# Layer 1 of a two-layer graph network: SyncE brings every 42nd chunk's rows

## The reference, cut to what matters

```python
N, E, D, R = 3750, 120000, 256, 8
h = relu(layernorm(x))                          # [N, D]
x = x + attention_layer(h, src, dst, type)      # layer 0: softmax over a node's incoming edges
h = relu(layernorm(x))
h_all = einsum('ni,rio->nro', h, W)             # [N, 8, 256]: one row for each (node, relation)
msgs = h_all[src, type]                         # one row of 256 floats (1 KB) for each edge
agg = segment_sum(msgs, dst)                    # summed by target node
g = gelu(agg + h @ loop_w + h_bias + h)
x = x + layernorm(g) * gamma + beta
```

## Time and profile before

| | us |
|---|---|
| median of 3 runs | 3214.21 |
| lowest and highest run | 3211.46, 3218.01 |
| span of the profiled execution, first to last instruction | 2765.4 |
| layer 1 within it, from POOL's first gather to the end | 1538.0 to 2765.4 |
| POOL, PE, DVE busy, whole span | 2027.0, 1916.5, 1521.9 |

### The profile page before, as it was taken

One profiled execution on the slowest core, in us unless ns is written; L12 is line 12 of the kernel. 1 busy time (PEld: TensorE's weight loads), 2 busy tenths in 40 slices (PEclk: granted clock), 3 DMA queues, 4 the chain that ended last, 5 costly groups with the idle time before them and its releaser, 6 DMA issues.

```text
span 2765.4 us, 26428 instructions
## 1 busy us (share of the span) xinstructions
PE 1916.5 (69%) x8092; PEld 1421.7 (51%) x8092; DVE 1521.9 (55%) x3172; ACT 672.9 (24%) x1246; POOL 2027.0 (73%) x2137
## 2 busy tenths in 40 slices
PE   7993577887878778787887656565655656565564
PEld 6992355555555555555555444444444444444443
DVE  6765677787777778777877423323332333333233
ACT  3753323443443344344331100000000000000001
POOL 5866777777777777777774577777777777777775
PEclk9995689899899999989999877768677776877777
DMA  8557456556565655656553533333333333333333
GB/s 224 228 195 233 137 151 177 168 173 179 163 183 169 177 168 172 179 163 185 169 161 89 170 105 105 105 110 105 110 107 109 111 105 110 105 110 110 106 111 94
DMA packets 168504, 403.11 MB, mean 146 GB/s; under 512 B 49741, under 2 KB 75820, under 8 KB 160682
## 3 DMA queue, kind: packets, MB, share of 16 engines
q0 software_dynamic: 95312, 261.58, 34.9%
q1 hardware_dynamic: 73050, 139.85, 14.5%
HBM read 325.41 MB, written 75.86 MB: 145 GB/s over the span
## 4 chain that ended last, share of the span: by engine, by line
POOL 49%; issue 18%; PE 17%; DVE 12%; DMA 3%; ACT 0%; DVEq 0%; POOLq 0%; ACTq 0%; SPq 0%
POOL Z L857 49%; PE PB L1910 7%; PE PB L1862 5%; DVE Z L1397 3%; DMA Z<-tab,KI 3%; DVE ACC L1369 3%; PE PB L2028 3%; PE PB L1986 1%; PE PB L1970 0%; PE PB L2071 0%; DVE EV L1411 0%; DVE E L1414 0%; DVE RV L1433 0%; DVE sf L1444 0%; POOL Z L805 0%
## 5 line engine op out<-in xcount | busy, mean ns | idle before, releaser
L857 POOL DMA_INDIRECT Z<-tab,KI x1963 | 1870.3, 953 | 658.7 <-issue 576.6
L1910 PE MATMUL PB<-Z,OHZ 128*128 128x260 f32 (+1 forms) x3926 | 1253.7, 484 | 528.2 <-DMA Z<-tab,KI 388.7
L1910 PEld LDWEIGHTS PB<-Z,OHZ 128*128 128x128 f32 x3926 | 941.3, 248 | 784.3 <-DMA Z<-tab,KI 415.2
L1369 DVE TENSOR_TENSOR ACC<-ACC,PB 128x260 f32 (+1 forms) x997 | 421.7, 423 | 851.6 <-PE PB L1910 826.5
L1397 DVE TENSOR_TENSOR Z<-Z,PB 128x2048 f32<-128x2048 f32 (+1 forms) x125 | 283.8, 2271 | 0.0
L2028 PE MATMUL PB<-w,ht 128*128 128x512 f32 x448 | 218.5, 644 | 12.8 <-ACT ht L1788 12.8
L1842 ACT ACTIVATE ACC<-ACC 128x256 f32<-128x256 f32 x30 | 10.4, 405 | 772.9 <-DVE ACC L1369 772.9
L1660 ACT ACTIVATE sd<-ve 128x1 f32<-128x1 f32 (+2 forms) x52 | 10.6, 203 | 660.7 <-DVE ve L1617 403.2
L2028 PEld LDWEIGHTS PB<-w,ht 128*128 128x128 f32 x448 | 89.3, 204 | 124.7 <-issue 105.5
L1862 PE MATMUL PB<-wh,hx 128*128 128x424 f32 (+1 forms) x500 | 145.1, 362 | 1.0 <-ACT hx L1674 1.0
L1387 DVE TENSOR_TENSOR OHZ<-DL,PB 128x1024 f32<-128x1024 bf16 (+1 forms) x122 | 140.2, 1210 | 0.1
(11 more groups left out here) (352 smaller groups left out, 1662.2 us busy)
## 6 DMA issues: line engine op xcount, KB each, us to landing
OHZ<-dlt SPq DMA_DIRECT2D x31, 1024.0 KB
Z<-tab,KI POOLq DMA_INDIRECT x1963, 2.8
tab<-st SPq DMA_DIRECT2D x120, 256.0 KB, 3.8
tab<-Z SPq DMA_DIRECT2D x24, 1040.0 KB, 4.1
TD<-typ SPq DMA_DIRECT2D x31, 256.0 KB
tab<-Z SPq DMA_DIRECT2D x5, 1024.0 KB, 7.2
xn<-xb SPq DMA_DIRECT2D x30, 128.0 KB, 3.3
X<-xn SPq DMA_DIRECT2D x6, 640.0 KB, 9.8
```

Source lines behind the costliest of these rows:

```text
L857: pool.indirect_dma_start(to, None, tab, at).then_inc(d_fe[g % 2][part(g, k) * layer], 16)
L1369: dv.tensor_tensor(a, a, bank(done + i)[:, 0:width], ALU.add).wait_op(*previous, "sem-ge").then_inc(*o.of(s_add))
L1910: last = pe.matmul(p, OH[:, slot, k + i, :], rows_, start=(i == 0), stop=(i == n - 1))
```

## The change

`BY_SP` is 46, 88, 130, ..., 928: 22 chunks. POOL leaves them out (`absent`). SP fetches each of them by 128 transfers of one row, from an address that stands in a register, to one partition of `LAND`, two tiles that lie over the first two rows of `rows`. The addresses are the keys in `ERM`, turned into integers and shifted left by 10 (1024 bytes a row) by two new DVE operations; SP loads 16 of them at a time. SP waits until PE has used the chunk brought two before. After a chunk's rows it stores those output blocks whose scaling falls in an earlier group than the chunk's; the rest are stored at the end. PE reads those chunks' rows from `LAND` and waits for them by a semaphore of their own, one of four.

```diff
+BY_SP = list(range(46, END1 - G, 42))
+    tab1b = tab1.rearrange("q f -> (q f)").bitcast(U8)
+        LAND = over("land", [128, 2, D], F32, rows_at)
+        KR = ERM[:, :].bitcast(I32)
+        def scaled_in(b):
+            return next(NB + 2 if then is None else then for a, c, ready, at, then in ENDS if a <= b < c)
         def absent(k):
-            return k < UNITS[0][0]
+            return k < UNITS[0][0] or k in BY_SP
+        def landed_by_sp(k):
+            i = BY_SP.index(k)
+            return d_sp[i % 4], 16 * 128 * (i // 4 + 1)
+        def row_bytes(e, engine, k, a, n):
+            return nc.values_load_multi_w_load_instructions(
+                KR[k % 128:k % 128 + 1, 128 * (k // 128) + a:128 * (k // 128) + a + n], engines=[engine], min_val=0, ...)[1]
         def rows1(g, k):
-            return FE[:, g % 2, k, 0:D]
+            c = GROUPS1[g][0] + k
+            return LAND[:, BY_SP.index(c) % 2, :] if c in BY_SP else FE[:, g % 2, k, 0:D]
 # SP, after X <- xn
+            done = 0
+            sp.wait_ge(s_kr, 1)
+            sp.wait_ge(s_o1, 1)
+            for i, k in enumerate(BY_SP):
+                if i > 1:
+                    sp.wait_ge(s_pair, NPAIR + unit_of(BY_SP[i - 2]) + 1)
+                for a in range(0, 128, 16):
+                    at = row_bytes(sp, SYE, k, a, 16)
+                    for p in range(a, a + 16):
+                        sp.dma_start(LAND[p:p + 1, i % 2, :].bitcast(U8), tab1b[bass.ds(at[p - a], 4 * D)].rearrange("(o n) -> o n", o=1)
+                                     ).then_inc(d_sp[i % 4], 16)
+                while done < NB and scaled_in(done) < k // G:
+                    store_output(done)
+                    done += 1
+            for b in range(done, NB):
+                store_output(b)
 # DVE, after KI
+            dv.tensor_copy(KR, ERM[:, :]).then_inc(*o.of())
+            dv.wait_ge(*o.last())
+            dv.tensor_scalar(KR, KR, 10, None, ALU.logical_shift_left).then_inc(*o.of(s_kr))
 # PE, before weigh
+                    for c in range(k, k + n):
+                        if c in BY_SP:
+                            pe.wait_ge(*landed_by_sp(c))
```

More of the change, by code:

```diff
@@ L33 @@
 BIG = float(2.0**100)
-F32, I32, BF16, FR = mybir.dt.float32, mybir.dt.int32, mybir.dt.bfloat16, mybir.dt.float32r
+F32, I32, BF16, FR, U8 = mybir.dt.float32, mybir.dt.int32, mybir.dt.bfloat16, mybir.dt.float32r, mybir.dt.uint8
 UPPER = -4096
@@ L362, in program @@
         d_out = sem("d_out")
+        d_sp = [sem(f"d_sp{i}") for i in range(4)]
+        s_kr = sem("s_kr")
         d_rows = sem("d_rows")
@@ L451, in part, with unit_of @@
             return c // 4 if g == len(GROUPS1) - 1 else c // 8
+        def scaled_in(b):
+            return next(NB + 2 if then is None else then for a, c, ready, at, then in ENDS if a <= b < c)
         def absent(k):
-            return k < UNITS[0][0]
+            return k < UNITS[0][0] or k in BY_SP
+        def unit_of(k):
+            return next(u for u, (a, n) in enumerate(UNITS) if a <= k < a + n)
+        def landed_by_sp(k):
[3 more added lines that the diff above has]
+            return nc.values_load_multi_w_load_instructions(
+                KR[k % 128:k % 128 + 1, 128 * (k // 128) + a:128 * (k // 128) + a + n], engines=[engine], min_val=0,
+                max_val=4 * D * (NB * 128 * NREL - 1), skip_runtime_bounds_check_because=
+                "the keys are numbers of the table's rows, times the bytes of a row")[1]
         def rows0(g):
@@ L756, in _, with store_output @@
                 sp.dma_start(X[:, b:b + 5, :], xn[b:b + 5].rearrange("b p f -> p b f")).then_inc(d_back, 16)
-            for b in range(NB):
+            def store_output(b):
                 t = block_rows(sp, SYE, b, out)
```

## The result

| kernel | median us | lowest, highest | runs |
|---|---|---|---|
| before | 3213.50 | 3211.46, 3218.01 | 4 |
| after | 3845.65 | 3825.53, 3853.24 | 4 |

The ratio is 1.1968, with a 95% interval of 1.1938 to 1.1998: 20% slower, where 3188 us was predicted and 3183 to 3345 was the range.

What follows compares the result with a forecast made beforehand. POOL's back-to-back gathers were taken to bound layer 1. Removing 22 at 1.254 us takes 27.6 us off the 2765.4 us span, 3214.2 us becoming 3186.6; with 1 us for joins 3188 us, range 3183 to 3345.

Steps and rivals of the forecast that it cites:

- What bounds layer 1: Layer 1: POOL issues gathers back to back at 1.254 us each; removing 22 saves 27.6 us, and POOL stays last.
- The 448.8 us outside the span are untouched.: Whole kernel: time beyond the profiled span of 2765.4 us stays, so the median is 3214.2 + (span - 2765.4).
- P: SP's time per chunk in layer 1: 8 register loads plus 128 row periods, 9.1 + 128 x 0.32 = 50.1 us.
- case 2: SP slightly slower than POOL, 0.33 to 0.345 us a row: saving eaten, within 0.2% of before; chance 0.06.
- its formula: The span when SP bounds layer 1: 1607 + 22 P, passing 2737.8 at P = 51.4 and 2765.4 at P = 52.7.
- The choice between 0.29 and 0.43 us a row: SP's row pitch: fixed address 0.29, both register operations 0.43; 0.32 us taken, with one light register operation.
- case 1: SP keeps pace, a row at most 0.33 us: span 2737.8, 3188 us with joins; chance 0.54.
- case 3: From 0.34 us a row SP bounds layer 1, PE waits for `LAND`, POOL for PE: 3259 to 3721 us; chance 0.33.
- Case 4: SP's load of a single row is dear in itself: 0.69 us a row, P = 97, 4190 us; chance 0.07.
- The one-engine form: SP's rows: all 128 transfers and semaphore writes of a chunk go through one DMA engine; 256 packets are 22 us.
- The rule on coalescing: SP's row transfers: many small transfers should be coalesced, as below 64 KB mostly overhead is paid; no price given.
- DVE's two operations and the joins: A conversion and a shift, about 2.6 us, hidden in DVE's wait for ACT; 1 us for joins at the new tiles.

Runs made afterwards that it cites:

- none: The changed kernel with nobody bringing the 22 chunks POOL leaves out, PE multiplying stale rows; 3180.97 us on the slow kind, ratio 0.9910 to before.
- one: The changed kernel with one fixed-address transfer of 128 rows per chunk instead of 128 transfers; 2733.56 us on the quick kind, ratio 0.9900 to before.
- again: The kernel before, unchanged, run again on the slow kind; 3212.07 us, ratio 1.0003.
- both_incs: Against `both`, 15 of every 16 row transfers with their MOVEs replaced by 30 semaphore increments; 3564.52 us on the slow kind, before 3205.94.
- after3: The changed kernel, unedited, on the quick kind; 2756.35 us, ratio 0.9987 to before.
- both: The changed kernel, but POOL gathers the 22 chunks too and PE uses POOL's rows; 3929.60 us on the slow kind, ratio 1.2242 to before.
- both_nogather2: Against `both`, POOL gathers nothing in layer 1 and PE multiplies stale tiles; 3000.41 us on the slow kind, before 3194.62.

## Why the prediction was wrong, step by step

- **What bounds layer 1.** Right: POOL's issuing. `none` and `one` gave 29 and 27 us for 22 gathers, and TensorE did not come next.
- **"The 448.8 us outside the span are untouched."** Wrong, and a sign missed. They weren't outside a span; they were the distance between two kinds of chip. 448.8 us unaccounted, a sixth of the span, should have been a rival of its own: the page of the profile is not of a chip of the kind that is timed, so its prices may not hold there. On the slow kind POOL has pauses, 359.8 us over the span in `again`, that the earlier trace rows lack:

```profile
POOL Z L857 <- remote: 359.8, 104, 11.8
```

- **P, the term that decided, is the step that failed.** Its size was wrong where it was timed: 50.1 us a chunk were put, 90.5 were measured. The sum took SyncE's time for a load and a row as the same whatever runs beside it, and so put the slowing beside POOL's gathers at nothing, without a reason. Worked out: 1.14 us a load with its gap, 0.32 a row, P = 50.1. On the quick kind: 1.30 a load with its gap, (6.58 - 1.30) / 16 = 0.330 a row, P = 52.6. That is the edge of case 2, and its formula holds: 1607 + 22 x 52.6 = 2764 for a span of 2759.2, and the stores and waits between the chunks took (2725.1 - 1550.2) - 22 x 52.6 = 17.7 us where 17 were put. On the slow kind P is some 160 us beside POOL, 53.5 alone, and 90.5 in after, where both alternate. The profile that was read had no hint of this: at line 705, beside POOL's gathers of layer 0, its register operations take 37 to 42 and 29 to 38 ns. The same line of the same kernel on the slow kind (`again`) has it:

```profile
L705 SPq FUSED_REGOPS  x116: 3/37/974, 471.3 to 1785.1; - x116
```

An operation of 37 ns that takes up to 974 is the sign, and it stood there before any change to the kernel.
- **The choice between 0.29 and 0.43 us a row.** One register operation of 29 ns stayed, as chosen. The middle was right to 0.01 us. But P stood 3% below 51.4, where the gain begins to shrink, and 5% below 52.7, where it is gone, and the chances should have been set by that: even on the quick kind it was case 2, given 0.06, and not case 1, given 0.54. Case 2 was also badly bounded: by the prediction's own formula 0.33 us a row still gives nearly the whole gain and 0.345 a loss of 13 us, 0.5%, which is not "within 0.2% of before".
- **The mechanism of the loss** is case 3's: PE waits for `LAND` (691.7 us), POOL for PE (664.6 us), the chain runs along SyncE. But no price of case 3 reached the P that was measured (its highest was 75.7), and none had the cause. By its own formula with P = 90.5 the span is 1607 + 1991 = 3598; SyncE's first row came at 1822.7 and not at 1550, which makes it 3871, for 3847.8 measured.
- **Case 4**, a single row dear in itself, is out: 0.225 us a transfer. That its P of 97 lies near the 90.5 measured is chance. The one-engine form can be read from the packets of the queue hardware_dynamic, 73050 in the kernel before. `after` has 78682, two more for each of its 2816 rows; `one` has 76218, 144 more for each of its 22 transfers of 128 rows, which is 128 and 16. So beside its data a row's transfer sends one packet, where a whole chunk's sends 16. The Trainium skill's page "DMA: Bandwidth & Descriptors" ("Why a DMA increments its semaphore by 16 and not by 1") has such a contiguous row spread over several engines where software splits it up. Here nothing does, and the counts agree with a single engine for each row. That it is always the lowest-numbered one no row here shows. As the cause of the loss it is excluded by `both_incs`, which keeps its slow pace with a sixteenth of the rows.
- **The rule on coalescing** of the Trainium skill's page "DMA: Bandwidth & Descriptors" ("Rules for kernel authors") came out right, though for a reason it doesn't give: one transfer of 128 rows (`one`, on the quick kind) keeps the whole saving, 128 transfers keep 4 of 27 us on that kind and lose 632 on the slow one. What was paid was SyncE's time per instruction, not the queue's per transfer.
- **DVE's two operations and the joins** cost nothing that the runs could tell: `one` has both and saves 27.2 of 27.6. The two operations take 0.68 and 0.69 us in `after3`, where 2.6 together were put, and 6.40 us of the wait for ACT are left behind them.

## What to carry to other kernels

When the profile's span and the timed median differ by more than a few us, find out why before adding terms: run the kernel before again with a profile, and take prices from that. Look there not only at medians but at the maxima of an engine's shortest instructions. Work given to an idle engine isn't priced by its rows on an idle chip alone; an engine's stream of short instructions has to be measured beside the engine that bounds the kernel, in a form in which nobody waits for it (`both`). And where the gain is capped and the loss isn't, give the helper much less than it can bear: 6 chunks gave their 7.5 us on the quick kind and cost nothing on the slow one, 22 gave 4 and lost 632.

## What the runs showed of the hardware

- Two kinds of chip, each chip met once: the same program at 2761 and at 3195 to 3218 us. On the slow kind a gather still takes POOL 0.95 us, but between its 967 gathers of layer 1 it stands still 29 times for 138.8 us with no releaser on the core (the row of `again` above), which is some 4.8 us each, about every 47 us. The quick kind has no such pause, and `both_nogather2`, without gathers, has none either (waits from 1830 to 2300). What distinguishes the chips no run tells.
- On the slow kind, beside POOL's gathers, SyncE executes an instruction every 0.6 to 0.7 us on the mean, be it a load, a MOVE, a transfer or a semaphore increment: 20.4 us for 33 instructions with 16 transfers, 19.4 us for 33 with one, 11 us for 16 transfers. Once the gathers are over the same batches take 6.7, 3.6 and 4.8 us, and the first takes 6.6 to 6.7 on the quick kind beside gathers. A quarter of the gathers' bytes in two thirds of their packets changes nothing; PE at 80% busy without gathers does nothing.
- Where nothing slows SyncE, a load of 16 registers takes it 1.25 us, a dynamic transfer of one row 0.225 with one MOVE of 0.029, 0.33 us from row to row.
